# Row tiles of every fourth row: four units of x per load in 2 KB stretches, and the strided turns, diagonal blocks and splits that follow from it

## The reference

```python
h = maximum(layernorm(x), 0)                 # over the last axis
A = relu((adj + adj.T) * 0.5)
D = A.sum(axis=1);  r = where(D > 0, D ** -0.5, 0)
L = eye(2048) - r[:, None] * A * r[None, :]
out = x + relu(einsum('nm,bmo->bno', L, einsum('bnf,fo->bno', h, W)))
```

## Time and profile before

| | |
|---|---|
| three executions, median (lowest to highest) | 401.59 us (401.29 to 401.61) |
| the profiled execution's own time, and its span | 401.33 us, 399.5 us |
| TensorE busy | 375.5 us (94%) |
| VectorE busy | 311.1 us (78%) |
| ScalarE busy | 192.5 us (48%) |
| GpSimd busy | 117.0 us (29%) |
| DMA packets | 69567, 55.00 MB |
| of these under 2 KB | 58272 |
| chain that ended last | PE 76%, DVE 14%, ACT 3%, issue 3%, DMA 2% |

### The profile page before, as it was taken

The page is one execution under the profiler, slowest core; times in us unless marked ns, Lnnn a source line. Parts: engine busy times, 40 slices in busy tenths (PEclk is TensorE's granted clock), DMA queues, the critical chain, the costliest instruction groups (busy, mean ns, idle before and its releaser), DMA issues.

```text
span 399.5 us, 6166 instructions
## 1 busy us (share of the span) xinstructions
PE 375.5 (94%) x2144; PEld 201.3 (50%) x2144; DVE 311.1 (78%) x606; ACT 192.5 (48%) x416; POOL 117.0 (29%) x253
## 2 busy tenths in 40 slices
PE   3568899989999999999999999999999999999995
PEld 3568854434444444545454445444544544454454
DVE  2868799788799887999879679967965796679246
ACT  1576876889976777867854133212211121113001
POOL 0496006678678245453511120400000000000000
PEclk9998999999999999999999999999999999999999
DMA  8999997012325431342254049921130122012203
GB/s 256 387 388 386 384 279 218 26 53 64 97 80 191 151 106 54 112 153 80 80 184 132 26 122 345 298 79 54 53 106 2 53 77 83 2 53 79 80 27 107
DMA packets 69567, 55.00 MB, mean 138 GB/s; under 512 B 2848, under 2 KB 58272, under 8 KB 69536
## 3 DMA queue, kind: packets, MB, share of 16 engines
q1 hardware_dynamic: 69536, 54.60, 42.8%
HBM read 39.91 MB, written 14.68 MB: 137 GB/s over the span
## 4 chain that ended last, share of the span: by engine, by line
PE 76%; DVE 14%; ACT 3%; issue 3%; DMA 2%; SPq 1%; DVEq 0%; ACTq 0%
PE ps L1256 11%; PE ps L1258 10%; PE ps L1257 10%; PE ps L1246 10%; PE ps L1240 10%; PE ps L1241 10%; PE ps L1154 4%; DVE S L846 3%; DMA S<-in_adj_dram 2%; DVE stats L803 2%; DVE S L819 2%; PE ps L1191 2%; PE ps L1292 2%; PE ps L1294 2%; PE ps L1293 2%
## 5 line engine op out<-in xcount | busy, mean ns | idle before, releaser
L1240 PE MATMUL ps<-S,hbuf 128*128 128x512 f16 x240 | 91.0, 379 | 1.4 <-ACT S L695 1.4
L1241 PE MATMUL ps<-S,hbuf 128*128 128x512 f16 x240 | 91.0, 379 | 0.0
L1246 PE MATMUL ps<-S,hbuf 128*128 128x512 f16 x256 | 76.2, 379 | 0.1
L1256 PE MATMUL ps<-S,hbuf 128*128 128x512 f16 x152 | 57.6, 379 | 0.0
L1257 PE MATMUL ps<-S,hbuf 128*128 128x512 f16 x152 | 57.6, 379 | 0.0
L1258 PE MATMUL ps<-S,hbuf 128*128 128x512 f16 x152 | 57.6, 379 | 0.0
L735 ACT ACTIVATE g<-ps 128x512 f16<-128x512 f32 x31 | 18.3, 595 | 68.0 <-DVE ps L926 32.0
L674 ACT ACTIVATE ps<-hbuf,lnt 128x128 f32<-128x128 f32 x112 | 44.9, 449 | 4.9 <-DVE hbuf L809 4.9
L846 DVE SCALAR_TENSOR_TENSOR S<-S,dneg 128x512 f16<-128x512 f32 x54 | 40.1, 753 | 5.6 <-ACT S L695 5.4
L1246 PEld LDWEIGHTS ps<-S,hbuf 128*128 128x128 f16 x256 | 25.0, 98 | 30.6 <-DVE S L846 1.1
L695 ACT ACTIVATE S<-S,dneg 128x512 f16<-128x512 f32 x54 | 37.5, 716 | 5.9 <-DVE S L846 4.2
(11 more groups left out here) (143 smaller groups left out, 693.8 us busy)
## 6 DMA issues: line engine op xcount, KB each, us to landing
S<-in_adj_dram SPq DMA_DIRECT2D x15, 1024.0 KB, 14.5
hbuf<-in_x_dram SPq DMA_DIRECT2D x64, 128.0 KB, 3.1
sums<-in_x_dram SPq DMA_DIRECT2D x32, 256.0 KB, 2.9
out_dram<-sums SPq DMA_DIRECT2D x31, 256.0 KB, 2.3
t_forms<-work SPq DMA_DIRECT2D x24, 256.0 KB, 3.1
S<-t_forms SPq DMA_DIRECT2D x5, 1024.0 KB, 9.6
S<-in_adj_dram SPq DMA_DIRECT2D x2, 512.0 KB, 13.4
S<-t_forms SPq DMA_DIRECT2D x1, 768.0 KB, 9.7
```

The lines of the kernel that those rows point to most:

```text
L1240: nc.tensor.matmul(acc, hbuf[:, u, 0, at:at + P], l_hi(t), start=(i == 0), stop=False)
L1241: nc.tensor.matmul(acc, hbuf[:, u, 1, at:at + P], l_hi(t), start=False, stop=False)
L1246: last = nc.tensor.matmul(acc, hbuf[:, u, 0, at:at + P], l_lo(t), start=False, stop=(i == T - 1))
L1256: nc.tensor.matmul(acc, a_hi, b_hi, start=starts, stop=False)
```

## The change

The rows of a tile are dealt out anew: row `512 g + 4 p + k` now stands in tile `4 g + k`, partition `p`. So a partition's rows in the four tiles of a group follow each other in memory. From this come the following edits:

- `adj` is loaded with the same 2 KB pieces, but from rows `4p + k`; its columns keep their order.
- The first sixteen units of x are loaded four units at a time: two DMAs of 512 KB in 2 KB pieces (`load_four`) in place of eight of 128 KB in 512-byte pieces, with one semaphore for four units. The four units lie together, and a unit is read from that with a step of 2 KB between its four blocks. The reloads of later units stay with 512-byte pieces, but a reload waits until all four units of its group are used, and is issued at the slot of the last of them.
- `sums` and the results are moved in 2 KB pieces; the two last stores in pieces of 1 KB.
- The turns read the stationary tile of `S` with a step of four float32 (16 bytes) and write PSUM with the same step.
- `take_diag` reads and writes its block of `S` with a step of four.
- `split_g_hi` and `split_g_lo` read the PSUM bank with a step of four and write `g16` tile by tile. For the last tile's halves the step is two, and the moving operand of its matmuls and the sum before take two of every four columns.

The diff, cut to its core:

```diff
+    x_v = x.rearrange("(h b) (i v p k) f -> h v k i p b f", b=PAIR, i=PAIR, p=P, k=GRP)
+    x_fours = x.rearrange("(h b) (i v p k) f -> h v i p b (k f)", b=PAIR, i=PAIR, p=P, k=GRP)
+    x_rows = x.rearrange("b (g p i) f -> b g p (i f)", i=GRP, p=P)
+    out_rows = out.rearrange("b (g p i) f -> b g p (i f)", i=GRP, p=P)
+    adj_v = adj.rearrange("(i p k) m -> i p k m", k=GRP, p=P)
+    def tile_cols(n):
+        return slice(WIDE * (n // GRP) + n % GRP, WIDE * (n // GRP + 1), GRP)
+    def by_tiles(cols, tiles=GRP):
+        return cols.rearrange("p (c k) -> p k c", c=P, k=tiles)
+    def tiled(cols, tiles=GRP):
+        return cols.rearrange("p (k c) -> p k c", c=P, k=tiles)
+    def half_cols(cols, h):
+        return cols.rearrange("p (c h k) -> p h c k", h=2, k=GRP // 2)[:, h]
...
+            def load_four(v):
+                for i in range(PAIR):
+                    half = x_four(v)[:, PAIR * i * WIDE:PAIR * (i + 1) * WIDE].rearrange("p (b f) -> p b f", b=PAIR)
+                    sp.dma_start(half, x_fours[GRP * v // UNITS, v % (UNITS // GRP), i]).then_inc(x_in[v], 16)
...
             def reload_x(k):
-                sp.wait_ge(h_hi_ready, k + 1)
-                wait_h_lo(sp, k + 1)
+                four = k // GRP * GRP
+                sp.wait_ge(h_hi_ready, four + GRP)
+                wait_h_lo(sp, four + PAIR)
+                wait_h_lo(sp, four + GRP)
...
                 for k in range(UNITS, 2 * UNITS):
-                    if h_slot[k] == tau:
+                    if h_slot[k // GRP * GRP + GRP - 1] == tau:
                         reload_x(k)
...
-                nc.scalar.activation(g16[:, e % 2, 0, :], ps[:, acc_bank(e), :], ACT.Copy,
+                nc.scalar.activation(tiled(g16[:, e % 2, 0, :]), by_tiles(ps[:, acc_bank(e), :]), ACT.Copy,
                                      scale=G_SCALE).then_inc(g_hi_ready, 1)
...
-                d = S[:, mt, mt * P:(mt + 1) * P]
+                d = S[:, mt, tile_cols(mt)]
...
-                nc.vector.scalar_tensor_tensor(g16[:, e % 2, 1, :], ps[:, acc_bank(e), :], G_SCALE, g16[:, e % 2, 0, :],
+                nc.vector.scalar_tensor_tensor(tiled(g16[:, e % 2, 1, :]), by_tiles(ps[:, acc_bank(e), :]), G_SCALE,
+                                               tiled(g16[:, e % 2, 0, :]),
                                                ALU.mult, ALU.subtract).then_inc(g_lo_ready, 1)
...
-                    last = nc.tensor.transpose(ps[:, k, q * P:(q + 1) * P], S[:, GRP * i + q, n * P:(n + 1) * P], ident[:])
+                    last = nc.tensor.transpose(ps[:, k, tile_cols(q)], S[:, GRP * i + q, tile_cols(n)], ident[:])
...
-                nc.tensor.matmul(acc, a_hi, b_hi[:, cols], start=starts, stop=False)
+                nc.tensor.matmul(acc, a_hi, half_cols(b_hi, h), start=starts, stop=False)
```

More of the change, by code:

```diff
@@ L146, in tile_of, with half_flat @@
         return PAIR * q + b, 2 + j
[L148 to L151, removed]
+    x_v = x.rearrange("(h b) (i v p k) f -> h v k i p b f", b=PAIR, i=PAIR, p=P, k=GRP)
[11 more added lines that the diff above has]
+        return cols.rearrange("p (c h k) -> p h c k", h=2, k=GRP // 2)[:, h]
+    def half_flat(cols):
+        return cols.rearrange("p (c k) -> p c k", k=GRP // 2)
     t_forms = nc.dram_tensor("t_forms", (3, HALF, P, 2 * WIDE), F16, kind="Internal").ap()
@@ L198, in gnn_layer, with x_four, x_buf, xn_buf @@
         T_BANK, XN_BANK = 4, 5
[L200 to L206, removed]
+        def x_four(v):
+            u = 2 * UNITS + GRP * v
+            return hbuf[:, u:u + GRP].rearrange("p u c w -> p (u c w)").bitcast(F32)
+        def x_buf(u):
+            if u < 2 * UNITS:
+                return x_four(u // GRP).rearrange("p (q k f) -> p q k f", k=GRP, f=P)[:, :, u % GRP, :]
+            return hbuf[:, u].rearrange("p c w -> p (c w)").bitcast(F32).rearrange("p (q f) -> p q f", f=P)
+        def xn_buf(u):
+            return x_buf(u) if u < EARLY else ps[:, xn_bank(u), :].rearrange("p (q f) -> p q f", f=P)
+        def h_buf(u, part):
+            return hbuf[:, u, part, :].rearrange("p (q f) -> p q f", f=P)
         def xn_bank(u):
@@ L291, in gnn_layer @@
         w_in = sem("w_in")
-        x_in = [sem(f"x_in{u}") for u in range(2 * UNITS)]
+        x_in = [sem(f"x_in{v}") for v in range(2 * UNITS // GRP)]
         x2_in = [sem(f"x2_in{s}") for s in range(4)]
@@ L458, in store_sums @@
                 sp.wait_ge(sum_ready, e + 1)
[L459 to L460 removed]
+                sp.dma_start(out_rows[b, g], sums[:, e % SUMS, :]).then_inc(out_done[e % SUMS], 16)
             def load_adj(i, j):
@@ L475, in _ @@
                     load_adj(j, i)
[L476 to L480, removed]
+                for v in range(EARLY // GRP):
+                    if x_step[GRP * v] == s:
+                        load_four(v)
+            for v in range(EARLY // GRP, 2 * UNITS // GRP):
+                load_four(v)
             for e in range(SUMS):
@@ L536, in _ @@
             b, g = tile_of(TILES - 1)
-            last_sums = sums[:, (TILES - 1) % SUMS, :].rearrange("p (i f) -> p i f", i=GRP)
+            last_sums = sums[:, (TILES - 1) % SUMS, :]
             for h in range(2):
-                rows = slice(h * GRP // 2, (h + 1) * GRP // 2)
+                rows = slice(h * WIDE // 2, (h + 1) * WIDE // 2)
                 sp.wait_ge(sum_ready, TILES + h)
@@ L673, in normalise @@
                     c = u % LN_BATCH * GRP + b
-                    last = nc.scalar.activation(xn_buf(u, b, b + 1), x_buf(u, b, b + 1), ACT.Relu,
+                    last = nc.scalar.activation(xn_buf(u)[:, b], x_buf(u)[:, b], ACT.Relu,
                                                 bias=neg_mean[:, c:c + 1], scale=y[:, c:c + 1])
@@ L802, in statistics @@
                 for b in range(b0, b1):
-                    last = nc.vector.bn_stats(stats[:, u % LN_SLOTS, b, :], x_buf(u, b, b + 1))
+                    last = nc.vector.bn_stats(stats[:, u % LN_SLOTS, b, :], x_buf(u)[:, b])
                 if b1 == GRP:
@@ L1190, in turn_mirror @@
                 for q in range(GRP):
-                    last = nc.tensor.transpose(ps[:, 4 + k, q * P:(q + 1) * P], S[:, GRP * j + q, r * P:(r + 1) * P], ident[:])
+                    last = nc.tensor.transpose(ps[:, 4 + k, tile_cols(q)], S[:, GRP * j + q, tile_cols(r)], ident[:])
                 last.then_inc(m_turned, 1)
@@ L1306, in last_part @@
                 acc, cols = last_acc(h)
-                nc.tensor.matmul(acc, a_hi, b_hi[:, cols], start=starts, stop=False)
-                nc.tensor.matmul(acc, a_hi, b_lo[:, cols], start=False, stop=False)
-                last = nc.tensor.matmul(acc, a_lo, b_hi[:, cols], start=False, stop=ends)
+                nc.tensor.matmul(acc, a_hi, half_cols(b_hi, h), start=starts, stop=False)
+                nc.tensor.matmul(acc, a_hi, half_cols(b_lo, h), start=False, stop=False)
+                last = nc.tensor.matmul(acc, a_lo, half_cols(b_hi, h), start=False, stop=ends)
                 if ends:
```

29 lines of the change are left out of this document (14 added, 15 removed).

## The result

The kernel after takes 405.98 us (median of 5, 405.40 to 406.16) against 401.34 (401.29 to 401.61) for the kernel before beside it: a ratio of 1.0112, 95% interval 1.0101 to 1.0124. That is 4.6 us slower, where the prediction's sum was 0.8 us faster (400.6 us), and 1.5 us above the upper end of its range. Its profiled execution took 405.92 us, with a span of 404.1 us against 399.5.

The account below looks back on a forecast made before the run. Bound: a front of about 60 us set by adj's arrival, then TensorE at full pace, then a short tail. Sum -0.87 (x) -0.1 (last store) +0.2 (steps) = -0.8 us, so 400.6 us; range 399.9 to 404.5.

Parts of the forecast that it names:

- x of the first four units: In the front, behind the first adj block: 1.05 MB at 387 instead of 293 GB/s, 0.87 us off.
- adj's own loads: In the front: same pieces from other rows; bounds -0.9 to +0.9 us (2% of 43 us), taken as 0.
- the prediction's rule: In the front: whatever moves all of adj's landings by d moves the front's end by d.
- SP's queue: Earlier issue of the second adj block gives nothing; late reloads, eight issues instead of two, 2.6 us, taken as 0.
- The ring of four spill slots: At the reloads: about nine slots of 1.3 us till first reuse cover the issues; without it, up to 2.6 us once.
- Turns: 256 turns in the front keep 109 ns each, strided load hidden; bounds 0 and 109 more ns each, taken as 0.
- rival C: In the front, the step slows the turns: 403.8 us at 163 ns, 413 at double; decides from 130 ns; chance 0.18.
- Diagonal blocks and splits: From 62 to 72 us and before 103 us on VectorE: steps cost 0 to 2.2 us (3.0 with ScalarE's), taken 0.2.
- rival B: Up to 103 us, the step halves VectorE and ScalarE: +1.2 to +2.0 us, say 402.8 us; chance 0.19.
- Tail: Last tile's 48 matmuls 0 (bounds 0 to 5.2 us), half splits 0 (0 to 0.5), last store -0.1 us.

Follow-up runs that it names:

- x alone: The reloads spread kernel with adj's rows, the turns and the diagonal blocks as in the kernel before: 400.70 us, ratio 0.9981.
- rows 64 KB apart: Kernel before with adj loaded in the same 2 KB pieces but from rows 8p + k, a block's partitions 64 KB apart: 402.05 us, one run.
- reloads spread: Kernel after with the last group's four reloads (units 28 to 31) issued at their own slots instead of all in one go: 404.47 us, ratio 1.0080.
- W and x ahead: The reloads spread kernel with W and the first four units of x issued ahead of adj's first block: 403.25 us, ratio 1.0047.
- first block by tiles: The reloads spread kernel with adj's first block issued as four DMAs, one per tile, instead of one: 403.05 us, ratio 1.0051.

## Why the prediction was wrong, by its own steps

**x of the first four units: right in kind and size.** -0.87 us of front was predicted, -0.89 came when nothing else in the front was changed (59.34 against 60.23), and 0.70 of it reached the end; the last tile's passes took the difference. The rate was 396 GB/s instead of 293 in the same window, with two DMAs in 2 KB pieces in place of eight in 512-byte pieces. Size of the piece and number of DMAs changed together and weren't tried apart.

**adj's own loads: the step that failed most.** It was bounded by 0.9 us either way, and taken as 0 "as the DMA engines' share, not the memory, is full". The share stays near full while the bytes fall (0.92 at 225 GB/s), so a full share says nothing about the rate of rows not yet seen. The rows cost 1.25 us alone and, beside the other parts, 2.05 of the front. Two per cent of the whole stream was the wrong form for the bound: the loss arises in the first block or two.

It isn't only a loss of rate. From 2 to 10 us the kernel after moved as much as the kernel before (315 against 316 GB/s), x's gain making up for adj's loss. In the traces a load raises its semaphore in 16 steps, and the turns wait for the sixteenth: at step 6, 40.65 us, the turns at 40.74. In the kernel before the 16 steps of the first block come within 0.5 us of each other (5.49 to 5.96). In the kernel after fourteen come by 6.69 us and the other two at 7.92 and 8.42, and at later blocks too the last two come well behind the rest. So the table takes, at the last block of step 6, the eighth step (how far the bulk is) and the sixteenth (what TensorE waits for), in us:

| kernel | eighth | sixteenth | first product | from sixteenth to product |
|---|---|---|---|---|
| before | 39.30 | 40.65 | 60.23 | 19.58 |
| x alone | 38.36 | 39.76 | 59.34 | 19.58 |
| adj's rows alone | 40.30 | 42.35 | 61.93 | 19.58 |
| rows 64 KB apart | 39.96 | 41.39 | 60.95 | 19.56 |
| turns alone | 39.22 | 40.72 | 60.97 | 20.25 |
| after, adj's old rows | 38.40 | 40.03 | 60.28 | 20.25 |
| after | 39.19 | 42.06 | 62.33 | 20.27 |
| reloads spread | 38.94 | 42.07 | 62.35 | 20.28 |
| W and x ahead | 39.05 | 41.14 | 61.42 | 20.28 |
| first block by tiles | 39.28 | 40.79 | 61.08 | 20.29 |

The last column has two values, 19.6 and, with the turns' step, 20.3 us. So the prediction's rule holds to 0.04 us: what moves adj's landings moves the front's end by as much. The front's 2.1 us are 1.41 of landing and 0.69 of turns. The landing's 1.41 is not the bulk, which is 0.11 us earlier than before, but the lag of the last step behind it, 2.87 us instead of 1.35. W and x ahead and the first block by tiles gained by this lag alone (2.09 and 1.51); their bulk is 0.1 and 0.3 us later than with spread reloads. Why the new rows hold up a few pieces at the start is open.

**SP's queue: the cover was counted wrongly.** The ring of four spill slots was said to have "about nine slots of 1.3 us till its first reuse". SP's queue in the kernel before, and the spills' times from issue to landing there, from 120 to 140 us:

```profile
122.76 0.47 SPq L459 DMA_DIRECT2D out_dram<-sums  x1
125.28 0.37 SPq L453 DMA_DIRECT2D sums<-in_x_dram  x1
125.75 1.45 SPq L497 DMA_DIRECT2D t_forms<-work  x3
```
```profile
DMA to landing us min/median/max: 3.1/3.2/3.4
```

In the kernel after ScalarE starts 3.24 us behind the issue of the first spill (133.23 to 136.47). By that its slot was free at 129.0 us in the kernel before, and ScalarE needs it at 130.24: some 1.2 us of cover. The spills are now issued 7.5 us later, 3.1 of them ScalarE's own lag and 4.4 the queue's. Of these 4.4, the eight issues make 3.1 (4.02 us where two took 0.88), the wait of `load_sums` for the store behind them 0.9 (3.4 us instead of 2.5), and a later start of the reloads 0.3. The prediction had 2.6 for the issues and left the longer wait out, though it named the queue's store. The cover took 1.2 of the 4.4 and ScalarE the rest, 3.1. "If this cover is gone, it costs up to 2.6 us once" was the right kind of sentence with the wrong chance: 1.5 us came.

**Turns: 0 was taken, 0.63 us came.** The pass's pace of 109 ns covered the load at 140 ns, as read, but not one at 211: 121 ns a turn (that the load sets the pace is read from these numbers; the write alone changed neither). The doubling of the streaming part was foreseen ("by some 50 ns") and said to "still lie beneath 109"; it didn't. The pace stays under the 130 ns from which rival C was to decide, yet the front lost 0.76 us (60.99 against 60.23): seven groups from 40 us on lose 0.19 us each, 1.3 in all, and only the idle 0.57 us at 48.85 covers any of it. The rival's place was right and its point of decision too high. The Trainium skill (SBUF — State Buffer, Specifications (TRN2)) has SBUF read in lines of 16 bytes that want at least two hits each; a step of four float32 hits each line once. The runs agree, for TensorE's load and for VectorE (367 to 470 ns). The rule on PSUM in the Trainium skill (Advanced Engine Details and Errata, Memory Cachelines), weighed in the prediction, doesn't hold here: the write with a step cost nothing (1.91 us for 16 turns, in one run).

**Diagonal blocks and splits: the term was mis-sized.** 0.2 us was taken. The splits, the larger part of rival B, cost nothing (687 and 595 ns). The diagonal cost 0.10 us a block, near the upper bound of 0.13, and eight of them came out at the stop near 89 us as 0.6 to 0.9. The argument that VectorE takes less than one element per ns anyway was wrong for SBUF and right for PSUM.

**Tail: right in size.** The steps in the last tile's 48 passes were taken as 0 and cost 0.2 us: some 4 ns of pace each, 113 instead of 109. The last stores gave back the 0.1 us that was predicted.

**The sum.** From the kernel after, spreading the reloads takes 1.5 us off and the first block by tiles 1.4: 403.05, 1.65 over before. That is -0.70 (x), +0.63 (turns), +0.94 (diagonal) and +0.8 (what the rows still cost in the front): +1.67. These are medians of single parts, so that the two sums agree to 0.02 us is partly luck. The parts measured alone on the kernel before (-0.70 + 1.25 + 0.63 + 0.94 + 0.58) make 2.7 of the 4.6 us. The rest is that the rows and the reloads cost more together with the other parts: 2.2 (405.98 - 403.75) against 1.25, and 1.5 against 0.58.

For the rows the semaphore steps show where. Each of these traces has one transfer of 16 KB on the instructions' own DMA queue that begins between 27 and 30 us and takes some 1.1 us. In the kernel before the last step's lag goes from 0.3 to 1.4 us with the next landing. In the kernel after it goes from 2.0 to 2.9 us; with the rows alone it stays at 2.0, as the lag then grows on other steps. That this transfer is the cause is argued from the times, not tried. For the reloads most of the gap is which executions are compared: in the profiled ones the matmuls slip at the stop by 1.64 us in the kernel after and by 1.22 with the reloads alone. What is left of it may be the lag of the diagonal blocks that ScalarE and VectorE bring with them, which wasn't tried by itself.

No version here that computes the reference's product beats the kernel before: the gain of 0.7 us needs the new rows of adj with it, and the turns' and the diagonal's steps alone cost 1.6.

## What to carry to other kernels

A layout that makes one transfer's pieces bigger puts a step into every other reader of the same rows; price each reader from the side of the memory that it reads, and don't let a small transfer (here 1 MB of 17.9) pay for steps on the chain. Where several short DMA issues are drawn together on one queue, follow the first item behind them to the engine that waits for its buffer, landing and all, in microseconds and not in slots. A bound on an unseen access order should be put on the rate of a stretch, not as a per cent of the whole stream. And a load is worth what its last semaphore step is worth: where engines wait for a landing, read the spread of its 16 steps beside the GB/s.

## What the runs showed of the hardware

- The first block of `adj`, the same 512 stretches of 2 KB each time, moved at 408 GB/s from 3 to 5 us when a partition's four rows lay 1 MB apart and neighbouring partitions' 8 KB; at 225 (270 in a second kernel with the same loads, 262 beside smaller pieces of x) when a partition took four consecutive rows and the partitions lay 32 KB apart; and at 321, followed by a us at 225, when the latter came as one DMA per tile. From 12 to 16 us on such rows moved at 387 as well. Why only the first block or two are slow stays open.
- Two of the 16 semaphore steps of that block came at 7.92 and 8.42 us, the other fourteen by 6.69, and the last step came 2.0 to 2.9 us behind the eighth in each of the next 13 blocks. Of the 2 KB pieces begun from 3 to 5 us the median took 84 ns, and 30 of 220 took over 200 ns, the longest 0.68 us; with the old rows none of 398 did.
- The load of a 128 x 128 float32 stationary tile took 140 ns contiguous and 211 with a step of 16 bytes, and the pace of transposes went from 109 to 121 ns. Their write to PSUM with that step took nothing (1.91 us for 16 of them in one run, as before).
- VectorE took 103 ns more for 128 x 128 float32 in SBUF with a step of 16 bytes, but ScalarE and VectorE read 512 float32 of PSUM with that step at their old 595 and 687 ns.
- Behind TensorE's two stops near 89 us, of 0.32 and 1.52 us, the granted clock was 0.58 from 90 to 94 us, the lower level of 1.2 GHz for most of it, in the profiled executions of two kernels (the diagonal alone; the kernel after with adj's old rows), and 1.00 in those of the four others with the same stops. It cost some 1.3 us there.
